# Eight of a chunk's 64 source columns come by one-hot products, a feed-forward layer changes its stationary side, and the end runs in two halves

## The reference, cut to what matters

```python
h = (x_flat @ W_gat).reshape(M, HEADS, NUM_EXPERTS)
e = leaky_relu(a_src[src] + a_dst[dst], 0.2)
ee = exp(e - segment_max(e, dst)[dst]); denom = segment_sum(ee, dst)
msg = h[src] * (ee / (denom[dst] + 1e-16))[:, :, None]
agg = segment_sum(msg, dst).reshape(M, 16) + b_gat
scores = layernorm(agg).reshape(M, HEADS, NUM_EXPERTS).mean(1)
# the two best experts of four, softmax over their scores
for ei in range(4):
    out = out + g[..., None] * (gelu(x @ W1[ei] + b1[ei]) @ W2[ei] + b2[ei])
```

## Time and profile before

| | us |
|---|---|
| runs of the kernel: lowest, median, highest | 7069.25, 7080.68, 7084.65 |
| profiled execution: its own time | 7082.19 |
| its span | 7080.3 |
| sort, up to about | 1270 |
| four images and preparation, up to the first gather | 3771.3 |
| gather stage, first to last gather | 3771.3 to 6612.3 |
| carry, scatter, 128 node gathers, up to | 6848 |
| node arithmetic | 6848 to 6910 |
| mix, up to the end | 6910 to 7080 |
| busy: PE, PEld | 3038.4, 1892.7 |
| busy: DVE, ACT, POOL | 3408.1, 1543.1, 2604.6 |

### The profile page before, as it was taken

The page is one execution under the profiler, slowest core; times in us unless marked ns, Lnnn a source line. Parts: engine busy times, 40 slices in busy tenths (PEclk is TensorE's granted clock), DMA queues, the critical chain, the costliest instruction groups (busy, mean ns, idle before and its releaser), DMA issues.

```text
span 7080.3 us, 84805 instructions
## 1 busy us (share of the span) xinstructions
PE 3038.4 (43%) x32141; PEld 1892.7 (27%) x32141; DVE 3408.1 (48%) x6941; ACT 1543.1 (22%) x3954; POOL 2604.6 (37%) x2472
## 2 busy tenths in 40 slices
PE   0011149866987888788750222222222222222205
PEld 0011138524852674377330000000000000000104
DVE  9999988576857685776661111111111111111128
ACT  0000037313730562165200111111111111111100
POOL 0000000050011000100017777777777777777450
PEclk9965579876987898698855565655555555656557
DMA  2000040002000200010022222222222222222207
GB/s 81 0 0 0 0 167 4 4 19 55 4 11 1 40 3 1 21 9 3 1 33 22 33 33 33 33 33 33 33 33 33 31 29 32 33 33 33 59 7 255
DMA packets 259741, 227.82 MB, mean 32 GB/s; under 512 B 115037, under 2 KB 222986, under 8 KB 250314
## 3 DMA queue, kind: packets, MB, share of 16 engines
q0 software_dynamic: 78944, 29.28, 6.7%
q1 hardware_dynamic: 99818, 99.91, 4.6%
q10 hardware_dynamic: 80640, 93.86, 4.3%
...
## 4 chain that ended last, share of the span: by engine, by line
PE 27%; another core or an unknown queue 19%; DVE 18%; issue 17%; DVEq 7%; DMA 4%; POOL 4%; ACT 4%; ACTq 1%; SPq 0%; POOLq 0%
DVE SA_ L1315 3%; PE PSB L1167 3%; PE PSB L382 3%; DVE SA_ L1305 2%; PE PSB L527 2%; PE PSB L679 2%; POOL SA_ L955 2%; POOL VPAD L965 2%; PE PSB L352 2%; DMA VPAD<-s_TNT 2%; DVE SA_ L583 2%; PE PSB L392 2%; DVEq L1396 2%; PE PSB L661 1%
## 5 line engine op out<-in xcount | busy, mean ns | idle before, releaser
L955 POOL DMA_INDIRECT SA_<-s_T,GIX x2048 | 2167.0, 1058 | 675.5 <-issue 675.5
L1167 PE MATMUL PSB<-VPAD,EH 128*128 128x512 f32 x512 | 303.4, 758 | 1995.3 <-DMA VPAD<-s_TNT 1818.0
L900 DVE TENSOR_TENSOR XPAD<-SA_ 128x256 f32<-128x256 f32 x32 | 13.6, 426 | 1790.8 <-DMA SA_<-s_T,GIX 1790.8
L947 POOL DMA_INDIRECT s_AEXP<-fill,SIX x128 | 149.6, 1169 | 1554.9 <-DVE SA_ L580 1468.1
L1167 PEld LDWEIGHTS PSB<-VPAD,EH 128*128 128x128 f32 x512 | 122.5, 248 | 2197.5 <-DMA VPAD<-s_TNT 1861.0
L851 POOL DMA_INDIRECT SA_<-s_SK,BLKI x128 | 132.2, 1033 | 1483.2 <-PE PSB L703 1396.3
L1171 PE MATMUL PSB<-SA_,EW 128*128 128x512 f32 x512 | 346.1, 825 | 341.4 <-issue 202.0
L1419 PE MATMUL PSB<-ident,SA_ 128*128 128x128 f32 x448 | 81.8, 364 | 837.9 <-DVE SA_ L1386 576.4
L303 ACT ACTIVATE PRX<-PSB,MX 128x144 f32<-128x144 f32 x1024 | 377.3, 381 | 210.8 <-DVE MX L224 210.6
L1156 ACT ACTIVATE VPAD<-PSB,PRX 128x512 f32<-128x512 f32 x128 | 88.2, 689 | 1308.1 <-remote 916.5
L1152 ACT ACTIVATE SA_<-PSB,PRX 128x512 f32<-128x512 f32 x256 | 176.4, 689 | 771.5 <-remote 319.9
...
## 6 DMA issues: line engine op xcount, KB each, us to landing
SA_<-s_T,GIX POOLq DMA_INDIRECT x2048
...
```

The lines of the kernel that those rows point to most:

```text
L955: pool.indirect_dma_start(out=n.G[:,s,c,:],out_offset=None,in_=d["T"],in_offset=IOA(ap=n.GIX[s][:,c:c+1],axis=0)).then_inc(n.gath[s],16)
L1167: pe.matmul(PSB[:,(m%4)*512:(m%4+1)*512],n.WM1[:,m//2,(m%2)*P:(m%2+1)*P],n.TNC[:,s,:],start=True,stop=True).then_inc(n.moe_h,1)
```

## The change

- Of each chunk POOL gathers columns 0 to 55 (CG is 56). Columns 56 to 63 (TB is 8) come from the table in SBUF. A source number is split in its low ten and its upper bits; node n lies at partition n%128, column n//128. Per column TensorE spreads the low parts over all partitions (spread_pe), VectorE compares them with each partition's eight candidates (mask_dve), TensorE multiplies the eight one-hot masks with the table, 320 columns each (column_pe), and VectorE picks one of 16 groups of 20 by the upper bits and sums (pick_dve). The columns of chunk j+1 are made during chunk j: six before VectorE waits for the gathers of chunk j, two while it waits for the exponentials.
- TensorE's order mixes columns and experts; the experts have two hidden and two output banks instead of four and four. ScalarE does the experts of a chunk ahead of its exponentials and store.
- In feed-forward the second layer's weights are stationary, and the bias is added by ScalarE. The result is transposed by TensorE, behind all the groups' products, and VectorE adds it from PSUM.
- node and mix run twice, on half the nodes each, and each half waits for its own 64 node gathers.

```diff
+NH=NODES//128//2; HALFTMP=66*NH; TB=8; CG=CH-TB; TCOLS=TB*(NCH+3)
 edges_prep_dve:
+    mine=s(I,1).rearrange("p (j c) -> p j c",c=CH)[:,:,CG:]; lo,hi=n.LOF[:,0:TB*NCH],n.HIF[:,0:TB*NCH]
+    dve.tensor_scalar(lo.bitcast(i32)...,mine,1023,None,ALU.bitwise_and)
+    dve.tensor_scalar(hi.bitcast(i32)...,mine,10,None,ALU.logical_shift_right)
...
+def mask_dve(dve,n,PSB,at,q):
+    o=(4+q%2)*512
+    dve.wait_ge(n.tg_bc,at*TB+(q+1))
+    dve.tensor_tensor(n.OHT[q%2],PSB[:,o:o+P].unsqueeze(1).to_broadcast((P,8,P)),n.JC.unsqueeze(2).to_broadcast((P,8,P)),ALU.is_equal).then_inc(n.tg_oh,1)
+def pick_dve(dve,n,PSB,at,s,q):
+    o=(6+q%2)*512
+    dve.wait_ge(n.tg_mm,at*TB+(q+1))
+    dve.scalar_tensor_tensor(out=n.PK[:,q%2],in0=n.IOT.unsqueeze(2).to_broadcast((P,16,20)),scalar=n.HIF[:,bass.ds(at*TB+q,1)],in1=PSB[:,o:o+320]...,op0=ALU.is_equal,op1=ALU.mult).then_inc(n.tg_pk,1)
     dve.drain()
+    dve.tensor_reduce(n.G[:,s,CG+q,:],n.PK[:,q%2].rearrange("p h k -> p k h"),AX.X,ALU.add)
+def column_dve(dve,n,PSB,at,s,q):
+    pick_dve(dve,n,PSB,at,s,q)
+    if q+2<TB: mask_dve(dve,n,PSB,at,q+2)
+    else: mask_dve(dve,n,PSB,at+1,q+2-TB)
 edges_dve, chunk j:
+            lower_dve(dve,n,j+2,s); dve.drain()
+            for q in range(TB-2): column_dve(dve,n,PSB,j+1,1-s,q)
             dve.drain()
-            dve.wait_ge(n.gath[s],i*(CH*16)+CH*16)
+            dve.wait_ge(n.gath[s],i*(CG*16)+CG*16)
...
             dve.tensor_tensor(FW[:,0],FW[:,0],RB[:,1:CH+1,0:4],ALU.subtract).then_inc(n.fw_rdy,1)
+            for q in range(TB-2,TB): column_dve(dve,n,PSB,j+1,1-s,q)
             dve.wait_ge(n.fw_exp,j+1)
 edges_act:
-            for s in range(2): chunk(i,s); experts_act(act,n,PSB,d,i,s)
+            for s in range(2): experts_act(act,n,PSB,d,i,s); chunk(i,s)
 edges_pool:
-            for c in range(CH):
+            for c in range(CG):
+def spread_pe(pe,n,PSB,ident,at,s,q):
+    o=(4+q%2)*512
+    if not (isinstance(at,int) and q<2): pe.wait_ge(n.tg_oh,at*TB+(q-1))
+    pe.matmul(PSB[:,o:o+P],n.LOC[s][:,q:q+1].to_broadcast((P,P)),ident,start=True,stop=True).then_inc(n.tg_bc,1)
+def column_pe(pe,n,PSB,ident,at,s,q):
+    o=(6+q%2)*512
+    pe.wait_ge(n.tg_oh,at*TB+(q+1))
+    if not (isinstance(at,int) and q<2): pe.wait_ge(n.tg_pk,at*TB+(q-1))
+    for j in range(8): last=pe.matmul(PSB[:,o:o+320],n.OHT[q%2][:,j,:],n.TBN.rearrange("p (h j) k -> p j h k",j=8)[:,j],start=(j==0),stop=(j==7))
+    last.then_inc(n.tg_mm,1)
+    if q+2<TB: spread_pe(pe,n,PSB,ident,at,s,q+2)
+    else: spread_pe(pe,n,PSB,ident,at+1,1-s,q+2-TB)
+    def both(i,s):
+        j=i*2+s
+        for q in range(TB):
+            column_pe(pe,n,PSB,ident,j+1,1-s,q)
+            if q<4:
+                for m in (2*q,2*q+1): hidden_pe(pe,n,PSB,j,s,m)
+            elif q<6:
+                for e in (2*q-8,2*q-7): expert_pe(pe,n,PSB,j,e)
 l0ffn_pe:
-        for i in range(4):
-            pe.matmul(o,ones[0:1,:],n.B2R[:,:],start=True,stop=False)
-            for m in range(4): last=pe.matmul(o,n.HTL[:,g%2,m,i*P:(i+1)*P],n.W2[:,m,:],start=False,stop=(m==3))
+        for m in range(4): last=pe.matmul(PSB[:,(6+g%2)*512:(7+g%2)*512],n.W2[:,m,:],n.HTL[:,g%2,m,:],start=(m==0),stop=(m==3))
...
+    pe.wait_ge(n.s_gs,b+1)
+    for g in range(8):
+        pe.wait_ge(n.s_ya,b*8+(g+1))
+        if g>=2: pe.wait_ge(n.s_yg,b*8+(g-1))
+        for i in range(4): last=pe.transpose(PSB[:,o:o+P],n.Y[:,512*g+P*i:512*g+P*(i+1)],ident)
+        last.then_inc(n.s_yt,1)
 the end:
-            node_dve(dve,n,m.SA)
-            mix_dve(dve,n,PSB)
+            for h in range(2): node_dve(dve,n,m.SA,h); mix_dve(dve,n,PSB,h)
-            node_act(act,n,m.SA)
-            mix_act(act,n,out,m.tick)
+            for h in range(2): node_act(act,n,m.SA,h); mix_act(act,n,out,m.tick,h)
-        pool.indirect_dma_start(out=n.RE[:,t,:],...).then_inc(n.re_g,16)
+        pool.indirect_dma_start(out=n.RE[:,t,:],...).then_inc(n.re_g[t//NH],16)
-    dve.wait_ge(n.re_g,16*NT)
+    dve.wait_ge(n.re_g[h],16*NH)
```

More of the change, by code:

```diff
@@ L475, in l0ffn_dve @@
         if g: dve.drain(); Ln.stats(dve,n,range(4*g-4,4*g))
-        dve.wait_ge(n.s_ya,b*8+(g+1))
-        for t in range(4*g,4*g+4):
-            dve.scalar_tensor_tensor(out=n.X[:,t,:],in0=n.Y[:,t,:],scalar=n.GS[:,t:t+1],in1=n.X[:,t,:],op0=ALU.mult,op1=ALU.add)
+        dve.wait_ge(n.s_yt,b*8+(g+1))
+        for i in range(4):
+            t=4*g+i; o=g%2*512+i*P
+            last=dve.scalar_tensor_tensor(out=n.X[:,t,:],in0=PSB[:,o:o+P],scalar=n.GS[:,t:t+1],in1=n.X[:,t,:],op0=ALU.mult,op1=ALU.add)
+        last.then_inc(n.s_yg,1)
     dve.drain()
@@ L1010, in stage @@
             j=i*2+s
-            if not (isinstance(i,int) and i==0): sp.wait_ge(n.gath[s],i*(CH*16)); sp.sem_inc(tick,1); sources(i,s)
+            if not (isinstance(i,int) and i==0): sp.wait_ge(n.gath[s],i*(CG*16)); sp.sem_inc(tick,1); sources(i,s)
             sp.wait_ge(n.rbs[s],i+1); sp.sem_inc(tick,1)
@@ L1103, in node_dve @@
     dve.tensor_reduce(VR,T16,AX.X,ALU.add); dr()
[L1104 to L1105 removed]
+    dve.tensor_scalar(VR,VR,1.0/16,1e-5,ALU.mult,ALU.add).then_inc(n.nd_dve,1)
+    dve.wait_ge(n.nd_act,h*3+2)
     dve.reciprocal(VR,VR); dr()
@@ new lines, in expert_pe @@
+def expert_pe(pe,n,PSB,j,e):
+    pe.wait_ge(n.moe_ge,j*8+(2*e+2))
+    if e==0: pe.wait_ge(n.moe_ev,j*4+1)
+    if e>=2: pe.wait_ge(n.moe_ev,j*4+e)
+    for f in range(2): last=pe.matmul(PSB[:,(2+e%2)*512:(3+e%2)*512],n.WM2[:,2*e+f,:],n.HM2[:,2*e+f,:],start=(f==0),stop=(f==1))
+    last.then_inc(n.moe_ys,1)
+def spread_pe(pe,n,PSB,ident,at,s,q):
+    o=(4+q%2)*512
+    if not (isinstance(at,int) and q<2): pe.wait_ge(n.tg_oh,at*TB+(q-1))
+    pe.matmul(PSB[:,o:o+P],n.LOC[s][:,q:q+1].to_broadcast((P,P)),ident,start=True,stop=True).then_inc(n.tg_bc,1)
@@ new lines, in column_pe, with edges_pe, experts, columns @@
+def column_pe(pe,n,PSB,ident,at,s,q):
[6 more added lines that the diff above has]
+    else: spread_pe(pe,n,PSB,ident,at+1,1-s,q+2-TB)
+def edges_pe(pe,n,PSB,ident,V):
+    def experts(i,s):
+        j=i*2+s
+        for m in range(8): hidden_pe(pe,n,PSB,j,s,m)
+        for e in range(4): expert_pe(pe,n,PSB,j,e)
+    def both(i,s):
+        j=i*2+s
+        for q in range(TB):
[4 more added lines that the diff above has]
+                for e in (2*q-8,2*q-7): expert_pe(pe,n,PSB,j,e)
+    def columns(i,s):
+        for q in range(TB): column_pe(pe,n,PSB,ident,i*2+(s+1),1-s,q)
+    pe.wait_ge(n.fe_rdy,1); pe.wait_ge(n.tbn_ld,16*4); pe.wait_ge(n.moe_w,112)
+    spread_pe(pe,n,PSB,ident,0,0,0); spread_pe(pe,n,PSB,ident,0,0,1)
+    for q in range(TB): column_pe(pe,n,PSB,ident,0,0,q)
+    with pe.Fori(0,NCK//2) as i:
+        with pe.If(i<V):
+            for s in range(2): both(i,s)
+        with pe.If(V<=i):
+            for s in range(2): experts(i,s)
+    with pe.Fori(NCK//2,NCH//2) as i:
+        with pe.If(i<V):
+            for s in range(2): columns(i,s)
@@ L1195, in mix_pe, with mix_dve @@
             last.then_inc(n.mix_tr,1)
-def mix_dve(dve,n,PSB):
-    with dve.Fori(0,NCK//MIX) as i:
+def mix_dve(dve,n,PSB,h):
+    k=NCK//MIX//2
+    with dve.Fori(h*k,(h+1)*k) as i:
         for s in range(MIX):
@@ L1206, in mix_dve, with mix_act @@
             last.then_inc(n.mix_dv,1)
-def mix_act(act,n,out,tick):
-    o=out.rearrange("(t p) c -> p t c",p=P)
-    with act.Fori(0,NCK//MIX) as i:
+def mix_act(act,n,out,tick,h):
+    o=out.rearrange("(t p) c -> p t c",p=P); k=NCK//MIX//2
+    with act.Fori(h*k,(h+1)*k) as i:
         for s in range(MIX):
@@ L1212, in mix_act @@
             act.dma_start(o[:,bass.ds((i*MIX+s)*4,4),:],n.X3C[s]).then_inc(n.mix_out[s],16)
-    for s in range(MIX): act.wait_ge(n.mix_out[s],NCK//MIX*16)
+    if h:
+        for s in range(MIX): act.wait_ge(n.mix_out[s],NCK//MIX*16)
 EDGES=524288; INVALID=NODES; NBLK=COLS//BLK; ROWBITS=12; BITS=19
```

136 lines of the change are left out of this document (72 added, 64 removed).

## The result

The kernel after took 7867.0 us (median of runs from 7854.7 to 7873.8), the kernel before 7077.0 beside it: a ratio of 1.112 [1.110, 1.114]. The forecast said 6,676 and its range ended at 7,400. The loss is in the gather stage.

What follows compares the result with a forecast made beforehand. POOL's gather issue, 1.40 us each, was taken to bound the gather stage, then the serial end. 7082.2 - 291 (chunks) - 34 (after last gather) - 69 (halves) - 12 (feed-forward) = 6,676 us; range 6,540 to 7,400.

Steps and rivals of the forecast that it cites:

- TensorE's signals arrive late beside gathers: Rival, gather stage: products beside gathers seen only after 5.6 us; chunks 125 to 150 us, total 8,100 to 8,900; chance 0.14.
- 52 us of 78.4 at 2.4 GHz: Gather stage, TensorE per chunk: eight columns 38 us plus experts 14.4, within the 78.4 us of 56 gathers.
- the 63 us for a buffer's turn: Gather stage: buffer free some 17 us after its gathers, then columns 0 to 5 and experts some 46; below 78.4.
- the sum's 80.5: Gather stage, per chunk: 78.4 + 1.0 VectorE delay + 1.1 low clock, against 89.6; 9.1 x 32 = -291 us.
- The counter-evidence: Against late signals: image 0's attention, 35 gathers beside 116 TensorE instructions in 50 us, VectorE's 52 waits averaging 0.28 us.
- The pitch: Gather stage: POOL issues gathers 1.40 us apart, so 56 take 78.4 us; stretches at 1.25 noted, then 70.
- the rival of 0.06: Gather stage, POOL at 1.25 us per gather: chunks of 72 to 75 us, total 6,410 to 6,510; chance 0.06.
- The added VectorE work: Gather stage: masks, picks and reduces, 18.3 us per chunk, delay gathers by 1.0 us, ends 0 and 7.
- The clock rival: Gather stage: clock stays low, TensorE becomes the bound, 109 us per chunk, total 7,588 us; chance 0.18.
- After the last gather: Last gather to scatter: last chunk's experts no longer stand ahead; 65.7 us becomes 31, -34 us, ends -40 and 0.
- The end in halves: Final node and mix on half the nodes, overlapping the second 64 gathers: 395 to 326 us, -69, ends -81 and -40.
- The feed-forward: Feed-forward: stationary second-layer weights save TensorE time, later transposes cost some back; net -3 us per image, -12, ends -76 and +20.

Runs made afterwards that it cites:

- job at 7,090: Job in which the unchanged kernel before takes about 7,090 us; the changed kernel took 7867.0 us in one, beside 7077.0 for the kernel before.
- job at 6,820: Job in which the unchanged kernel before takes about 6,820 us; the changed kernel, unaltered, took 6434.2 us in one, beside 6818.3 (0.943).
- The run with pauses: Changed kernel, but POOL waits after every 14 gathers until they have landed: 7326.1 us, beside 7096.0 for the kernel before.
- the gauge: Separate small kernel, computing nothing of the reference: trains of VectorE, ScalarE or TensorE instructions beside DMA streams; 1650.1 us in a job at 7,090, 1593.8 in one at 6,820.

## Why the prediction was wrong

The forecast took one rival for improbable (0.14) that came true: "TensorE's signals arrive late beside gathers". It named the right rows and the right price, 5.6 us per product. Its time was too high, 8,100 to 8,900, because it let POOL's stand be longer: a chunk of 125 to 150 us, where 112.5 were measured. The trace shows why: after a stand TensorE's records run on unheld for some 25 us (gathers resume at 4889.73, the long gap begins at 4915.7), and 10 us after the last gather all are free again.

**The step that failed** is "52 us of 78.4 at 2.4 GHz" of TensorE work and the 63 us for a buffer's turn. It costed instructions by their own durations and not by their distance beside gathers. By the distance the added 288 instructions on TensorE alone are 288 x 1.40 = 403 us if all of them were held, which no chunk has. What the runs showed in its place: in the job at 7,090 the chain of columns, experts and exponentials that was to take 63 us took the whole chunk, 112.5 for the sum's 80.5. VectorE's first instruction behind the gathers, L942, waited for none of them there (2.9 us of idle time in all), and POOL waited 45 us for VectorE. In the job at 6,820 the step was right: L942 waited 489.9 us for gathers, 15 per chunk, POOL for nobody, and a chunk took 72.7. The symptom stood in the trace of before: ScalarE's wait of 10.51 us beside TensorE records of 3.50.

**The counter-evidence was misread.** Image 0's attention has 35 gathers in 50 us beside 116 TensorE instructions with short waits, and the text said "What differs I can't say". A difference that can't be named is no ground for so low a chance. Those gathers come in groups of some 15 with waits between, 1.43 us apart on the mean, while the stage has 56 to 64 in a row. That this difference decides is not shown. The run with pauses has groups of 14, and its chunk of 96.4 us was still 24 us above the 72.7 of a job at 6,820, of which its three waits explain 6; and in the gauge some 90 gathers in a row, with nothing beside them, left the next 17 instructions of VectorE free.

**The pitch.** The forecast took 1.40 for POOL's pace, and 1.25 for the rival of 0.06. The 1.40 is a mean that goes with the jobs at 7,090: there the unchanged gather stage takes 88.8 us per chunk, in jobs at 6,820 81.7. And in the kernel after the gathers of a chunk stand 1.25 apart even at 7,090, so the sum's 78.4 was 70 to 72; the loss is behind them. In the jobs at 6,820 the saving of eight gathers was 9.0 us and the stage -289 (2614.3 to 2325.6), against the forecast's -291. The number agrees, the ground for it doesn't: 8 x 1.40 less 2.1 of costs was forecast, 8 x 1.28 = 10.2 less a fixed part of the chunk came. The 6,434 us measured there lie among the rival's 6,410 to 6,510, and its chunks of 72 to 75 us came; that the time agrees is luck, for the kernel that it starts from takes 6,818 us there and not 7,082.

**The added VectorE work** was forecast at 1.0 us per chunk between 0 and 7. It was 0: the changed kernel and the version with 56 gathers and no columns both have 72.7. The mask took 1.22 (1.23 forecast), the pick 0.55 (0.53), the reduce 0.82 (0.53). The Trainium skill ("SBUF — State Buffer", Who interferes with whom) has it that a VectorE instruction with at most one SBUF input outside the two-port modes doesn't contend with GpSimd. These runs agree: 72.7 us with the eight columns and without.

**The clock rival** (0.18) fell: 0.88 over the stage in the job at 6,820 and 0.73 even in the job at 7,090, where the rival needed under 0.59.

**After the last gather,** -34 was forecast. In jobs at 6,820 it is -9 (48.3 to 39.4). The 65.7 that the sum started from belong to the jobs at 7,090 (the version without columns has 65.1 there and 48.3 at 6,820), and the 31 that it ended at were 8 too few. In the job at 7,090 it is +65.

**The end in halves:** forecast -69; in jobs at 6,820 -70 (396.4 with 56 gathers, 326.5 after), the node half 36.8 us (37 forecast). In the job at 7,090 the half took 61.7, as long as the whole before, because its later part stands beside gathers with 1.40 us per instruction; -16.5 is what was left. The forecast had bounded this "by their own 30 us" on the gathers' side and not on VectorE's.

**The feed-forward:** forecast -3 per image, measured -6.4 (83.5 to 77.1 us from the first hidden product to the last accumulation, in jobs of both sorts), -26 in all. The sum of a job at 6,820, -289 - 9 - 70 - 26 = -394, stands beside 384 measured. The kernel before has no trace from such a job, so its stage there is taken from the version without columns.

Which jobs are at 7,090, what the limit is made of, and whether the gathers' distance decides (1.25 slows others, 1.40 might be its edge) stays open. One rival is untested. Every time on record comes with a span and a granted clock, that is from an execution whose events were recorded. That this recording holds the engines up in some jobs isn't ruled out, for no run here is without it.
